# A routed expert stage on one core: second products spread between the next steps' first products, results added one step later

## Chip, cores and metric

The kernel runs on one NeuronCore of a Trainium2 chip. The metric is the device time of one launch in microseconds (us), the median of several runs. Lower is better.

## What is computed

A two-layer graph network on 1250 nodes with 1024 features is followed by a feed-forward layer in which each row is sent to 2 of 8 experts. The change touches the experts alone. Cut to that part, the reference is:

```python
def _L0_ffn_ref(x, rw1, rb1, rw2, rb2, ew1, eb1, ew2, eb2):
    B, F, D, H, E, K = (4, 256, 1024, 256, 8, 2)
    t = x.reshape(b * f, d)
    logits = silu(t @ rw1 + rb1) @ rw2 + rb2
    vals, idx = top_k(logits, K)
    ...
    w = softmax(masked, axis=1)
    eh = silu(einsum('td,edh->teh', t, ew1) + eb1[None])
    eo = einsum('teh,ehd->ted', eh, ew2) + eb2[None]
    y = t + einsum('te,ted->td', w, eo)
```

The kernel computes eh and eo only for the two chosen experts of each row.

## The kernel before

The rows are sorted by expert into blocks of 128 slots. The stage takes 17 steps (NS). A step belongs to one expert and has two blocks (a big step, 256 rows wide) or one (a small step, 128 rows wide). The fixed list ORDER makes steps 0, 3, 5, 8, 11, 13 and 16 small and the ten others big. BLOCKS(s) is the number of blocks of step s, WIDE(s) its width. Almost every tile has two buffers, chosen by u = s % 2.

Each float32 factor is split into a high part, which ScalarE copies out, and a low part, which VectorE gets by subtraction; a product is then three matmuls: high by high, high by low, low by high. One step s is made of these parts:

- Loading: SyncE's queue loads the first weights (w_raw, w = 0) and the second ones (w = 1), 1 MB each, as soon as the low parts of step s-2 free the buffer (m_wlo). GpSimd's queue gathers the rows (x_rows, L2093) when the transposes of step s-2 are done (m_tx), and issues the scatters (L2086) that add o_rows of a step to the output. There the gather of step t stands behind the scatter of step t-5.
- Splitting the weights: w1_hi (ScalarE, L2176; it waits until the first products of step s-2 are done, m_g1) and w1_lo (VectorE, L2226); w2_hi (ScalarE, L2181) and w2_lo (VectorE, L2226 too).
- Turning (turn, L2118): 8 transposes for each block on TensorE, in four groups, into PSUM banks 0 and 1. ScalarE copies a group to xt_hi (L2186) and VectorE forms xt_lo (L2231), after which the bank is free (m_xlo), so that group 2 waits for xt_lo of group 0.
- First products (L2132): for each half j of the 256 hidden columns 24 matmuls into bank 2 + j. ScalarE makes hid of them (L2194), then hid_hi (L2201), and VectorE hid_lo (L2249).
- Second products (tail of TensorE, L2153): 12 matmuls of 512 columns for each block, in two groups of 6, each into a PSUM bank of its own (4 + 2b + half). A group of step s waits on m_out until VectorE has read the bank's result of step s-1.
- Results: ScalarE's shift writes the weighted bias into o_rows (L2210), once for each block, and VectorE adds the scaled bank to it (L2259), once for each group, which counts up m_out.

Each engine's order is written out by hand. The pipeline runs head(s) and then tail(s-1). On TensorE head(s) is: 24 first products, half of the transposes of step s+1, 24 first products, the other half; tail(s-1) is the block of second products. On ScalarE head(s) is w1_hi of step s+1, hid of half 0, two groups of xt_hi, w2_hi of step s, hid of half 1, two groups of xt_hi, hid_hi; then follows shift(s-1). On VectorE head(s) is w1_lo of step s+1, two groups of xt_lo, w2_lo of step s, two groups of xt_lo, hid_lo; then the results of step s-1. Before and among the first transposes TensorE runs matmuls whose results nobody reads (keep_busy, L1976).

Of the kernel before, what the change touches and what calls it, by code (L numbers as in the profile page):

```python
# [31 lines left out]
KT = D // 128  # L32
# [29 lines left out]
M = 256  # L62
SUB = M // 128
BIG, SMALL = 10, 7
NS = BIG + SMALL
# [12 lines left out]
HK = HID // 128  # L78
# [25 lines left out]
def build(nc, I, out):  # L104
    ctx = ExitStack()
    with ctx:
# [1924 lines left out]
        LATE = 5  # L2031
        w1_view, w2_view = I["L0_ffn_ew1"], I["L0_ffn_ew2"]
# [70 lines left out]
        def _(e):  # L2103
# [6 lines left out]
            def turn(s, u, q, groups=range(4)):  # L2110
                if groups[0] == 0:
                    for b in range(BLOCKS(s)):
                        e.wait_ge(m_xin[u][b], NTH(s, b))
                for g in groups:
                    e.wait_ge(m_xlo, 4 * s + g + 1)
                    for k in range(2):
                        for b in range(BLOCKS(s)):
                            mm = e.transpose(ps[:, g % 2, k * M + 128 * b:k * M + 128 * b + 128],  # L2118
                                             x_rows[:, u, b, 128 * (2 * g + k):128 * (2 * g + k + 1)], ident[:])
                    mm.then_inc(m_tx, 1)  # L2120


            def head(s, u, q):
                e.wait_ge(m_wlo[0], s + 3)
                e.wait_ge(m_xlo, 4 * s + 4 + 2)
                for j in range(HK):
                    e.wait_ge(m_h, HK * s + j + 1)
                    n = 0
                    for k in range(KT):
                        for wt, xt in ((w1_hi, xt_hi), (w1_hi, xt_lo), (w1_lo, xt_hi)):  # L2130
                            n += 1
                            mm = e.matmul(ps[:, 2 + j, 0:WIDE(s)], wt[:, u, k, 128 * j:128 * j + 128], xt[:, u, k, 0:WIDE(s)],  # L2132
                                          start=(n == 1), stop=(n == 3 * KT))
                    mm.then_inc(m_g1, 1)
                    if not isinstance(s, int) or s < NS - 1:
                        turn(s + 1, 1 - u, q + u, range(2 * j, 2 * j + 2))
                if s == 0:
                    slot_weights(e)

            def tail(s, u, q):  # L2140
                if s == 1:
                    e.wait_ge(g_sl, 1)
                e.wait_ge(m_hlo, s + 1)
                e.wait_ge(m_wlo[1], s + 3)
                for b in range(BLOCKS(s)):
                    for half in range(2):
                        if s > 0:
# [159 lines left out]
```

## Time and profile before

| what | value |
|---|---|
| median of 3 runs | 1111.09 us |
| lowest and highest run | 1102.71 and 1113.34 us |
| span of the profiled execution, first to last instruction | 1107.6 us |
| difference between the median and that span | 3.5 us |
| mean granted TensorE clock in the span | 0.989 |
| the expert stage in it, from the first transpose (889.7 us) to the end | 217.9 us |

The page gives no time of the profiled execution beside its span. The rows further on come from this execution. A stretch is given in us from the start of the span. PE is TensorE, ACT ScalarE, DVE VectorE, POOL GpSimd, SP SyncE. The end of a matmul in the trace is modelled, so the distance from one start to the next is what it costs TensorE; "2.87 us x24" in the chain of waits is such a distance for 24 in a row.

### The profile page before, as it was taken

The page shows a single profiled execution, that of the slowest core. Times are in us where ns is not written, and L with a number is a line of the kernel's source. Part 1 is how long each engine was busy: PE and PEld are TensorE (multiplying, and loading weights), DVE is VectorE, ACT ScalarE, POOL GpSimd, SP SyncE. Part 2 cuts the span into 40 slices and gives each one's busy share as a digit, 9 for nine tenths or more (in the row PEclk, how much of TensorE's full clock was granted, in tenths as well). Part 3 has the DMA queues.
Part 4 walks back from the last instruction along what each step waited for, and adds up shares of the span by engine and source line. Part 5 has one row for each costly group of instructions (what it writes and reads, how often), then busy time and mean ns, then how long its engine had stood idle before and what let it go on. Part 6 is the DMA issues. An engine that isn't in the chain of part 4 may idle for free.

```text
span 1107.6 us, 18245 instructions
## 1 busy us (share of the span) xinstructions
PE 1068.1 (96%) x6565; PEld 1015.3 (92%) x6565; DVE 618.0 (56%) x1090; ACT 427.1 (39%) x934; POOL 193.4 (17%) x192
## 2 busy tenths in 40 slices
PE   5999999999999999999999999999999989999995
PEld 4999999999999999999999999999999679999994
DVE  6678888888752344334323523273222467878883
ACT  5555434453311222121121112164322257777672
POOL 5500000000000002000200020002442124555532
PEclk9999999999999999999999999999999979999998
DMA  6332133213227560004201430276565187999971
GB/s 191 95 105 71 44 108 108 70 43 105 71 71 242 148 186 16 1 19 150 67 1 54 129 76 1 58 244 189 158 186 190 38 302 233 318 304 291 304 220 29
DMA packets 72794, 144.97 MB, mean 131 GB/s; under 512 B 12822, under 2 KB 51667, under 8 KB 68209
## 3 DMA queue, kind: packets, MB, share of 16 engines
q1 hardware_dynamic: 61041, 112.50, 31.7%
q0 software_dynamic: 10976, 30.74, 10.7%
q8 instruction: 68, 1.11, 0.4%
q10 hardware_dynamic: 672, 0.32, 0.1%
q14 instruction: 37, 0.30, 0.1%
HBM read 108.40 MB, written 42.96 MB: 137 GB/s over the span
## 4 chain that ended last, share of the span: by engine, by line
PE 91%; DVE 3%; issue 2%; DMA 1%; DVEq 1%; ACT 1%; POOLq 0%; SPq 0%; POOL 0%; ACTq 0%
PE ps L1482 20%; PE ps L976 14%; PE ps L1554 10%; PE ps L2132 9%; PE ps L1521 9%; PE ps L1211 8%; PE ps L2153 6%; PE ps L821 4%; PE ps L735 3%; PE ps L2118 2%; PE ps L716 1%; DVE key_hot L814 1%; PE ps L921 1%; PE ps L1540 1%; DVE adj L828 1%
## 5 line engine op out<-in xcount | busy, mean ns | idle before, releaser
L1444 POOL TENSOR_TENSOR s_rows<-s_rows,b1t 125x1368 f32<-125x1368 f32 (+3 forms) x9 | 23.7, 2655 | 572.1 <-DMA s_rows<-in_x 572.1
L828 DVE TENSOR_TENSOR adj<-ps,adj 125x250 f32 x212 | 87.7, 414 | 42.0 <-PE ps L821 33.7
L976 PE MATMUL ps<-h_lo,w_hi 128*128 128x418 f32 x336 | 108.6, 372 | 0.0
L976 PE MATMUL ps<-h_hi,w_hi 128*128 128x418 f32 x336 | 100.3, 379 | 0.0
L1521 PE MATMUL ps<-z_hi,adj 125*125 125x342 f32 (+1 forms) x300 | 95.0, 322 | 1.4 <-DVE s_rows L1753 1.4
L1521 PE MATMUL ps<-z_lo,adj 125*125 125x342 f32 (+1 forms) x300 | 94.3, 319 | 0.0
L976 PE MATMUL ps<-h_hi,w_lo 128*128 128x418 f32 x336 | 93.4, 359 | 0.0
L2226 DVE TENSOR_TENSOR w_lo<-w_raw,w_hi 128x2048 fp32r<-128x2048 f32 x34 | 77.8, 2288 | 25.6 <-ACT w_hi L2181 20.8
L1211 PE MATMUL ps<-adj,y_hi 125*128 125x416 f32 (+1 forms) x240 | 85.8, 357 | 2.2 <-DVE layer_out L1276 1.6
L1211 PE MATMUL ps<-adj,y_lo 125*128 125x416 f32 (+1 forms) x240 | 85.4, 356 | 0.0
L821 PE MATMUL ps<-key_hot,src_hot 125*125 125x250 bf16 x424 | 80.8, 271 | 3.4 <-DVE adj L828 3.1
L2132 PE MATMUL ps<-xt_hi,w_hi 128*128 128x256 f32 (+1 forms) x272 | 78.4, 288 | 0.2
L2132 PE MATMUL ps<-xt_lo,w_hi 128*128 128x256 f32 (+1 forms) x272 | 77.5, 285 | 0.0
L2132 PE MATMUL ps<-xt_hi,w_lo 128*128 128x256 f32 (+1 forms) x272 | 77.5, 285 | 0.0
L1482 PE MATMUL ps<-wn_hi,hs_lo 128*125 128x342 f32 (+1 forms) x240 | 76.7, 320 | 0.0
L1482 PE MATMUL ps<-ws_hi,hs_hi 128*125 128x342 f32 (+1 forms) x240 | 76.7, 320 | 0.0
L1482 PE MATMUL ps<-wn_hi,hs_hi 128*125 128x342 f32 (+1 forms) x240 | 76.7, 320 | 0.0
L1482 PE MATMUL ps<-ws_lo,hs_hi 128*125 128x342 f32 (+1 forms) x240 | 76.7, 319 | 0.0
L1482 PE MATMUL ps<-ws_hi,hs_lo 128*125 128x342 f32 (+1 forms) x240 | 76.6, 319 | 0.0
L1482 PE MATMUL ps<-wn_lo,hs_hi 128*125 128x342 f32 (+1 forms) x240 | 76.5, 319 | 0.0
L821 PEld LDWEIGHTS ps<-key_hot,src_hot 125*125 125x125 bf16 x424 | 56.5, 136 | 18.7 <-issue 7.0
L814 DVE TENSOR_TENSOR key_hot<-seq,key_now 125x1000 bf16<-125x1000 f16 x106 | 71.2, 672 | 0.0
(301 smaller groups left out, 2685.6 us busy)
## 6 DMA issues: line engine op xcount, KB each, us to landing
w_raw<-in_L_ffn_ew SPq DMA_DIRECT2D x34, 1024.0 KB
xin<-in_x SPq DMA_DIRECT2D x10, 448.0 KB
t_d<-xn SPq DMA_DIRECT2D x10, 448.0 KB
base<-x_d POOLq DMA_DIRECT2D x10, 448.0 KB, 4.2
out<-base POOLq DMA_DIRECT2D x10, 448.0 KB, 3.5
y_d<-y_hi SPq DMA_DIRECT2D x7, 625.0 KB
y_d<-y_lo SPq DMA_DIRECT2D x7, 625.0 KB
self_d<-self SPq DMA_DIRECT2D x7, 625.0 KB
```

Source lines behind the costliest of these rows:

```text
L735: mm = e.matmul(FIRST_BANK(own, c)[:, a - COLS[c][0]:b - COLS[c][0]], wt[:, own, k, :], ht[:, k, a:b], start=(n == 0), stop=(n == 3 * KT - 1))
L814: ins = e.tensor_tensor(both(hot).rearrange("p c (v x) -> p c v x", x=2), seq, place, ALU.is_equal)
L821: mm = e.matmul(ps[0:P, 5 + b % 2, 0:KW], src_hot[:, b, g, 0:P], key_hot[:, b, g, :], start=(g == 0), stop=(g == G - 1))
L828: e.tensor_tensor(cols, ps[0:P, 5 + b % 2, 0:KW].rearrange("p (t w) -> p t w", t=NT), cols, ALU.add).then_inc(self.took, 1)
L976: mm = e.matmul(BANK(m, own, c), wt[:, own, k, :], ht[:, k, a:a + w], start=(k == 0 and p == 0), stop=(k == KT - 1 and p == 2))
L1211: mm = e.matmul(ps[:, banks[c], 0:w], y[:, k, :], adj_[:, k, a:a + w], start=(n == 1), stop=(n == 2 * NT))
L1482: mm = e.matmul(ps[0:P, 2 * v + u, 0:w], ht[:, u, k, :], wt[v][:, k, 0:w], start=(k == EARLY[0] and p == 0), stop=(k == LATE_K[-1] and p = ...
L1521: mm = e.matmul(ps[0:P, 2 + n % 2, 0:w], adj_[:, k, tile_of(j)], z[:, k, 0:w], start=(k == 0 and p == 0), stop=(k == NT - 1 and p == 1))
L1554: mm = e.matmul(ps[:, i % 5, 0:w], wt[u][:, k, :], ht[:, k, a:a + w], start=(n == 1), stop=(n == 3 * KT))
L2132: mm = e.matmul(ps[:, 2 + j, 0:WIDE(s)], wt[:, u, k, 128 * j:128 * j + 128], xt[:, u, k, 0:WIDE(s)], start=(n == 1), stop=(n == 3 * KT))
L2153: mm = e.matmul(ps[:, 4 + 2 * b + half, :], ht[:, u, j, 128 * b:128 * b + 128], wt[:, u, j, 512 * half:512 * half + 512], start=(n == 1), ...
L2226: e.tensor_tensor(lo[:, u], raw[:, u], hi[:, u].bitcast(F32), ALU.subtract).then_inc(m_wlo[i], 1)
```

## The change

On TensorE the two functions head and tail give way to single matmuls that are dealt out in turn. Iteration t has two phases of 24 first products of step t. In phase 0 (half j = 0) the second half of the second products of step t-2 is spread evenly between them. In phase 1 (j = 1) come the 16 or 8 transposes of step t+1, spread over the first 20 of the 24, and the first half of the second products of step t-1, spread over all 24. HALF(s) is 12 matmuls for a big step and 6 for a small one. Two more iterations at the end hold the second products that are left. The semaphore that each group of second products waits on (m_out) is the same as before. The first products of half 0 now wait for xt_lo group by group.

On VectorE the results of a step (outputs, formerly tail) are added one step later, inside head: after w1_lo of step s+1 and ahead of all four groups of xt_lo. w2_lo of step s comes behind the four groups. On ScalarE all four groups of xt_hi of step s+1 come behind hid of half 0, ahead of w2_hi of step s and hid of half 1. The queues of SyncE and GpSimd keep their order.

```diff
@@ -2029,6 +2029,7 @@
         NTH = lambda s, b: 16 * sum(i % 2 == s % 2 and b < BLOCKS(i) for i in range(s + 1))
         WIDE = lambda s: 128 * BLOCKS(s)
         LATE = 5
+        PRODUCTS, TURNING = 3 * KT, 20
         w1_view, w2_view = I["L0_ffn_ew1"], I["L0_ffn_ew2"]
 
         def gated(e):
@@ -2107,57 +2108,81 @@
             e.sem_inc(m_g1, 4)
             e.sem_inc(m_g2, 2 * NB)
 
-            def turn(s, u, q, groups=range(4)):
-                if groups[0] == 0:
-                    for b in range(BLOCKS(s)):
-                        e.wait_ge(m_xin[u][b], NTH(s, b))
-                for g in groups:
+            def turned(s, i):
+
+                u, B = s % 2, BLOCKS(s)
+                g, r = divmod(i, 2 * B)
+                k, b = divmod(r, B)
+                if i == 0:
+                    for c in range(B):
+                        e.wait_ge(m_xin[u][c], NTH(s, c))
+                if r == 0:
                     e.wait_ge(m_xlo, 4 * s + g + 1)
-                    for k in range(2):
-                        for b in range(BLOCKS(s)):
-                            mm = e.transpose(ps[:, g % 2, k * M + 128 * b:k * M + 128 * b + 128],
-                                             x_rows[:, u, b, 128 * (2 * g + k):128 * (2 * g + k + 1)], ident[:])
+                mm = e.transpose(ps[:, g % 2, k * M + 128 * b:k * M + 128 * b + 128],
+                                 x_rows[:, u, b, 128 * (2 * g + k):128 * (2 * g + k + 1)], ident[:])
+                if r == 2 * B - 1:
                     mm.then_inc(m_tx, 1)
 
-
-            def head(s, u, q):
-                e.wait_ge(m_wlo[0], s + 3)
-                e.wait_ge(m_xlo, 4 * s + 4 + 2)
-                for j in range(HK):
+            def product(s, j, n):
+
+                u = s % 2
+                k, p = divmod(n, 3)
+                wt, xt = ((w1_hi, xt_hi), (w1_hi, xt_lo), (w1_lo, xt_hi))[p]
+                if n == 0:
+                    e.wait_ge(m_wlo[0], s + 3)
                     e.wait_ge(m_h, HK * s + j + 1)
-                    n = 0
-                    for k in range(KT):
-                        for wt, xt in ((w1_hi, xt_hi), (w1_hi, xt_lo), (w1_lo, xt_hi)):
-                            n += 1
-                            mm = e.matmul(ps[:, 2 + j, 0:WIDE(s)], wt[:, u, k, 128 * j:128 * j + 128], xt[:, u, k, 0:WIDE(s)],
-                                          start=(n == 1), stop=(n == 3 * KT))
+                if j == 0 and n % 6 == 0:
+                    e.wait_ge(m_xlo, 4 * s + n // 6 + 1 + 2)
+                mm = e.matmul(ps[:, 2 + j, 0:WIDE(s)], wt[:, u, k, 128 * j:128 * j + 128], xt[:, u, k, 0:WIDE(s)],
+                              start=(n == 0), stop=(n == PRODUCTS - 1))
+                if n == PRODUCTS - 1:
                     mm.then_inc(m_g1, 1)
-                    if not isinstance(s, int) or s < NS - 1:
-                        turn(s + 1, 1 - u, q + u, range(2 * j, 2 * j + 2))
-                if s == 0:
+
+            def second(s, i):
+
+                u = s % 2
+                group, n = divmod(i, 3 * HK)
+                b, half = divmod(group, 2)
+                j, p = divmod(n, 3)
+                ht, wt = ((hid_hi, w2_hi), (hid_hi, w2_lo), (hid_lo, w2_hi))[p]
+                if i == 0:
+                    if s == 1:
+                        e.wait_ge(g_sl, 1)
+                    e.wait_ge(m_hlo, s + 1)
+                    e.wait_ge(m_wlo[1], s + 3)
+                if n == 0 and s > 0:
+                    e.wait_ge(m_out, GROUP_AT(s - 1) + 2 * NB + min(group + 1, 2 * BLOCKS(s - 1)))
+                mm = e.matmul(ps[:, 4 + group, :], ht[:, u, j, 128 * b:128 * b + 128],
+                              wt[:, u, j, 512 * half:512 * half + 512], start=(n == 0), stop=(n == 3 * HK - 1))
+                if n == 3 * HK - 1:
+                    mm.then_inc(m_g2, 1)
+
+            def share(n, of, total):
+
+                return range(min(n, of) * total // of, min(n + 1, of) * total // of)
+
+            HALF = lambda s: 3 * HK * BLOCKS(s) if 0 <= s < NS else 0
+            for i in range(8 * BLOCKS(0)):
+                turned(0, i)
+                if i == 4 * BLOCKS(0) - 1:
+                    keep_busy(e, 5)
+            keep_busy(e, 4)
+            for t in range(NS + 2):
+                turns = 8 * BLOCKS(t + 1) if t + 1 < NS else 0
+                for n in range(PRODUCTS):
+                    if t < NS:
+                        product(t, 0, n)
+                    for i in share(n, PRODUCTS, HALF(t - 2)):
+                        second(t - 2, HALF(t - 2) + i)
+                for n in range(PRODUCTS):
+                    if t < NS:
+                        product(t, 1, n)
+                    for i in share(n, TURNING, turns):
+                        turned(t + 1, i)
+                    for i in share(n, PRODUCTS, HALF(t - 1)):
+                        second(t - 1, i)
+                if t == 0:
                     slot_weights(e)
-
-            def tail(s, u, q):
-                if s == 1:
-                    e.wait_ge(g_sl, 1)
-                e.wait_ge(m_hlo, s + 1)
-                e.wait_ge(m_wlo[1], s + 3)
-                for b in range(BLOCKS(s)):
-                    for half in range(2):
-                        if s > 0:
-                            e.wait_ge(m_out, GROUP_AT(s - 1) + 2 * NB + min(2 * b + half + 1, 2 * BLOCKS(s - 1)))
-                        n = 0
-                        for j in range(HK):
-                            for ht, wt in ((hid_hi, w2_hi), (hid_hi, w2_lo), (hid_lo, w2_hi)):
-                                n += 1
-                                mm = e.matmul(ps[:, 4 + 2 * b + half, :], ht[:, u, j, 128 * b:128 * b + 128],
-                                              wt[:, u, j, 512 * half:512 * half + 512], start=(n == 1), stop=(n == 3 * HK))
-                        mm.then_inc(m_g2, 1)
-            turn(0, 0, 0, range(0, 2))
-            keep_busy(e, 5)
-            turn(0, 0, 0, range(2, 4))
-            keep_busy(e, 4)
-            skewed(e, NS, head, tail)
 
         def more(s):
             return not isinstance(s, int) or s < NS - 1
@@ -2192,9 +2217,9 @@
                 for j in range(HK):
                     wait_apart(e, m_g1, HK * s + j + 1 + 4)
                     e.activation(hid[:, u, j, 0:WIDE(s)], ps[:, 2 + j, 0:WIDE(s)], ACT.Silu, bias=eb1c[:, ds(x * HK + j, 1)]).then_inc(m_h, 1)
-                    if more(s):
-                        rows(s + 1, 1 - u, q + u, range(2 * j, 2 * j + 2))
                     if j == 0:
+                        if more(s):
+                            rows(s + 1, 1 - u, q + u)
                         w2(s, u, q)
                 e.wait_ge(m_h, HK * s + HK + 2)
                 e.wait_ge(m_g2, GROUP_AT(s - 1) + 2 * NB)
@@ -2241,16 +2266,17 @@
             def head(s, u, q):
                 if more(s):
                     w(0, w1_raw, w1_hi, w1_lo, s + 1, 1 - u, q + u)
-                    rows(s + 1, 1 - u, q + u, range(0, 2))
+                if s >= 2:
+                    outputs(s - 2, u)
+                if more(s):
+                    rows(s + 1, 1 - u, q + u)
                 w(1, w2_raw, w2_hi, w2_lo, s, u, q)
-                if more(s):
-                    rows(s + 1, 1 - u, q + u, range(2, 4))
                 e.wait_ge(m_hhi, s + 1)
                 e.tensor_tensor(hid_lo[:, u, :, 0:WIDE(s)], hid[:, u, :, 0:WIDE(s)], hid_hi[:, u, :, 0:WIDE(s)].bitcast(F32), ALU.subtract).then_inc(m_hlo, 1)
                 if s == 0:
                     slot_sums()
 
-            def tail(s, u, q):
+            def outputs(s, u):
                 for b in range(BLOCKS(s)):
                     e.wait_ge(m_eb, BLOCKS_TO(s) + b + 1)
                     for half in range(2):
@@ -2261,7 +2287,10 @@
             w(0, w1_raw, w1_hi, w1_lo, 0, 0, 0)
             rows(0, 0, 0)
             slot_shares(e)
-            skewed(e, NS, head, tail)
+            for s in range(NS):
+                head(s, s % 2, s // 2)
+            for s in range(NS - 2, NS):
+                outputs(s, s % 2)
 
 
         @on("sync")
```

TensorE around the start of the second products of step 1. m_out is the wait on VectorE's results. Before, they stand in one block behind both halves of the first products of step 2 (L2132) and all transposes of step 3 (L2118):

```order
L2132 MATMUL ps<-xt_hi,w_lo 128x256
L2118 MATMUL ps<-ident,x_rows 128x128 [waits m_xlo]
L2118 MATMUL ps<-ident,x_rows 128x128
L2118 MATMUL ps<-ident,x_rows 128x128 [waits m_xlo]
L2118 MATMUL ps<-ident,x_rows 128x128
L2153 MATMUL ps<-w_hi,hid_hi 128x512 [waits m_wlo1,m_out,m_hlo,g_sl]
L2153 MATMUL ps<-w_lo,hid_hi 128x512
```

Now the first of them (L2155) stands behind only two of the 24 first products of half 1 of step 2 (L2136; the one that waits on m_h is the first of the 24):

```order
L2136 MATMUL ps<-xt_hi,w_lo 128x256
L2155 MATMUL ps<-w_hi,hid_lo 128x512
L2136 MATMUL ps<-xt_hi,w_hi 128x256 [waits m_h,m_wlo0]
L2136 MATMUL ps<-xt_lo,w_hi 128x256
L2155 MATMUL ps<-w_hi,hid_hi 128x512 [waits m_wlo1,m_out,m_hlo,g_sl]
L2136 MATMUL ps<-xt_hi,w_lo 128x256
L2121 MATMUL ps<-ident,x_rows 128x128 [waits m_xlo,m_xin10]
L2136 MATMUL ps<-xt_hi,w_hi 128x256
L2155 MATMUL ps<-w_lo,hid_hi 128x512
```

What has moved: 22 first products and all transposes of that iteration now stand behind this wait instead of ahead of it.

VectorE, one step. Before, from the results of step 1 (two blocks, four additions L2259, each of which counts up m_out) to the xt_lo of the next step (L2231):

```order
L2249 TENSOR_TENSOR hid_lo<-hid,hid_hi 128x512 [waits m_hhi]
L2259 SCALAR_TENSOR_TENSOR o_rows<-ps,slot_w,o_rows 128x512 [waits m_g2,m_eb]
L2259 SCALAR_TENSOR_TENSOR o_rows<-ps,slot_w,o_rows 128x512 [waits m_g2]
L2259 SCALAR_TENSOR_TENSOR o_rows<-ps,slot_w,o_rows 128x512 [waits m_g2,m_eb]
L2259 SCALAR_TENSOR_TENSOR o_rows<-ps,slot_w,o_rows 128x512 [waits m_g2]
L2226 TENSOR_TENSOR w_lo<-w_raw,w_hi 128x2048 [waits m_whi0]
L2231 TENSOR_TENSOR xt_lo<-ps,xt_hi 128x512 [waits m_xhi] x2
```

Now the same additions (L2285), behind w1_lo, which waits for w1_hi of ScalarE (m_whi0):

```order
L2251 TENSOR_TENSOR w_lo<-w_raw,w_hi 128x2048 [waits m_whi1]
L2275 TENSOR_TENSOR hid_lo<-hid,hid_hi 128x512 [waits m_hhi]
L2251 TENSOR_TENSOR w_lo<-w_raw,w_hi 128x2048 [waits m_whi0]
L2285 SCALAR_TENSOR_TENSOR o_rows<-ps,slot_w,o_rows 128x512 [waits m_g2,m_eb]
L2285 SCALAR_TENSOR_TENSOR o_rows<-ps,slot_w,o_rows 128x512 [waits m_g2]
L2285 SCALAR_TENSOR_TENSOR o_rows<-ps,slot_w,o_rows 128x512 [waits m_g2,m_eb]
L2285 SCALAR_TENSOR_TENSOR o_rows<-ps,slot_w,o_rows 128x512 [waits m_g2]
L2256 TENSOR_TENSOR xt_lo<-ps,xt_hi 128x512 [waits m_xhi] x4
```

What has moved: one w1_lo now stands between hid_lo and the additions.

ScalarE now, from hid of half 0 (L2219) to the next w1_hi (L2201); before, two of the four xt_hi stood behind hid of half 1:

```order
L2219 ACTIVATE hid<-ps,eb1c 128x256
L2211 ACTIVATE xt_hi<-ps 128x2x128 [waits m_tx] x4
L2206 ACTIVATE w_hi<-w_raw 128x2048 [waits m_g2,m_win10]
L2219 ISA [waits m_g1]
L2219 ACTIVATE hid<-ps,eb1c 128x256
L2226 ACTIVATE hid_hi<-hid 128x512 [waits m_g2,m_h]
L2229 TENSOR_LOAD step_x
L2229 ISA x2
L2235 ISA [waits m_kept]
L2235 ACTIVATE o_rows<-eb_all,slot_w 128x1024
L2214 TENSOR_LOAD step_x
L2201 ACTIVATE w_hi<-w_raw 128x2048 [waits m_g1,m_win00]
```

What has moved: w2_hi (L2206) now stands behind the last xt_hi and ahead of hid of half 1.

## Rows read from the trace of the kernel before

**Rows 1.** The page, busy time, and the granted clock in 40 slices
```profile
PE 1068.1 (96%) x6565; PEld 1015.3 (92%) x6565; DVE 618.0 (56%) x1090; ACT 427.1 (39%) x934; POOL 193.4 (17%) x192
...
PEclk9999999999999999999999999999999979999998
```
**Rows 2.** Chain of waits in order of time: start us, us, what
```profile
893.66 2.87 PE ps L2132 x24
896.52 3.26 issue
899.78 1.94 PE ps L2118 x8
...
955.28 2.63 PE ps L2132 x24
957.91 0.90 PE ps L2118 x8
958.80 2.63 PE ps L2132 x24
...
962.33 5.49 PE ps L2153 x24
...
974.45 0.87 PE ps L2118 x8
975.33 2.77 PE ps L2153 x12
978.10 2.87 PE ps L2132 x24
```
**Rows 3.** ACT in order of time, one step
```profile
984.49 0.48 ACT L2194 ACTIVATE hid<-ps,eb1c 128x256 f32<-128x256 f32 x1 [0.48 <-PE ps L2132]
984.86 0.65 ACT L2186 ACTIVATE xt_hi<-ps 128x256 fp32r<-128x256 f32 x2
985.39 0.64 ACT L2201 ACTIVATE hid_hi<-hid 128x512 fp32r<-128x512 f32 x1
985.91 2.20 ACT L2210 ACTIVATE o_rows<-eb_all,slot_w 128x1024 f32 x2
987.99 1.92 ACT L2176 ACTIVATE w_hi<-w_raw 128x2048 fp32r<-128x2048 f32 x1
993.05 0.37 ACT L2194 ACTIVATE hid<-ps,eb1c 128x128 f32<-128x128 f32 x1 [3.13 <-PE ps L2132]
993.33 1.09 ACT L2186 ACTIVATE xt_hi<-ps 128x512 fp32r<-128x512 f32 x2
994.30 1.92 ACT L2181 ACTIVATE w_hi<-w_raw 128x2048 fp32r<-128x2048 f32 x1
```
**Rows 4.** DVE in order of time, one step
```profile
987.51 2.19 DVE L2259 SCALAR_TENSOR_TENSOR o_rows<-ps,slot_w,o_rows 128x512 f32<-128x512 f32 x3
990.24 0.75 DVE L2259 SCALAR_TENSOR_TENSOR o_rows<-ps,slot_w,o_rows 128x512 f32<-128x512 f32 x1 [0.54 <-PE ps L2153]
990.91 2.28 DVE L2226 TENSOR_TENSOR w_lo<-w_raw,w_hi 128x2048 fp32r<-128x2048 f32 x1
993.96 1.29 DVE L2231 TENSOR_TENSOR xt_lo<-ps,xt_hi 128x512 fp32r<-128x512 f32 x2 [0.77 <-ACT xt_hi L2186]
```
**Rows 5.** Stretches: us, busy PE, PEld, DVE, ACT, POOL, PEclk, DMA share, GB/s
```profile
347.00:353.00 6.00, 6.00 (x26) 5.79 (x26) 0.00 (x0) 0.00 (x0) 0.00 (x0) 0.72 0.88 255
896.50:899.80 3.30, 0.04 (x2) 0.05 (x1) 3.30 (x4) 0.37 (x1) 0.00 (x0) 0.74 0.80 305
899.80:914.00 14.20, 14.14 (x87) 13.91 (x88) 8.62 (x11) 6.66 (x8) 0.99 (x1) 0.58 0.80 298
1020.00:1040.00 20.00, 20.00 (x133) 18.16 (x132) 17.04 (x20) 13.73 (x17) 9.55 (x6) 1.00 1.00 310
```
**Rows 6.** PE in order of time, ahead of the first of these falls
```profile
344.99 2.34 PE L1259 MATMUL ps<-ones,dinv_row 1*125 1x1 f32 x20
```
**Rows 7.** Who waited for whom from 870 us: us in total, times, longest us
```profile
POOL x_rows L2093 <- PE ps L2118: 53.7, 15, 13.4
```
**Rows 8.** POOL in order of time, last scatter
```profile
1098.03 1.56 POOL L2086 DMA_INDIRECT out<-o_rows,ids_i  x1 [2.08 <-DMA out<-o_rows,ids_i]
```

## Prediction

> **What bounds the kernel now.** I read the page first: TensorE is busy for 96% of the span, at the full clock in all slices but one [rows 1]. The chain of waits then shows the expert stage as TensorE's work end to end. A big step is 24 first products in 2.87 us (0.12 each), twice; 8 transposes in 0.87 to 0.90 (0.11 each), twice; and second products in 0.23 each, 24 in 5.49 or 12 in 2.77. In a small step 24 first products take 2.63 [rows 2]. From 914 us to the last product this goes on without a gap. The only real hole in the stage is 3.26 us at 896.52, before the first transposes of step 1 [rows 2]. So TensorE is the bound, and the change neither adds nor removes a matmul. It can win only if mixing makes the same matmuls cheaper, and it can lose wherever an in-order wait comes too early. ScalarE and VectorE have waits today, but the reader should look at how long their chain from one step to the next is, not at their busy shares.
>
> The transfers are the other resource that is nearly full: a DMA share of 1.00 at 310 GB/s between 1020 and 1040 us [rows 5]. The change moves no issue on SyncE's or GpSimd's queue, but their releases come with VectorE's and TensorE's work. GpSimd waits for transposes for 53.7 us in 15 times [rows 7], so the gathers have room, and if steps get longer all loads get more. I count them at nothing. If that cover went, the price would be a wait like the 3.26 us one.
>
> **What the change makes late.** Call zero of iteration t the end of the last first product of step t-1. In phase 1 the first second product of step t-1 stands behind two first products (four, if t-1 is small) and waits on m_out for the first result of step t-2. VectorE adds that result only behind w1_lo of step t+1; that needs w1_hi of step t+1, which ScalarE does behind hid half 1 and hid_hi of step t-1 and the bias rows of step t-2. Before, the same bank had been read a whole step earlier in VectorE's order, and the block of second products (5.49 us) gave this chain its room.
>
> The chain, from starts to next starts: hid to hid_hi, with its own write to wait for, 0.5; hid_hi to bias rows 985.39 to 985.91, 0.52; bias rows 985.91 to 987.99, 1.04 a block; w1_hi 1.92 [rows 3]; w1_lo 2.25, first addition 0.75 [rows 4]; handing over 0.1. That is 6.05 + 1.04 per block of step t-2.
>
> It starts late as well. ScalarE's w2_hi now stands between the last xt_hi and hid half 1. The last transpose stands behind the 20th first product. From its end ScalarE needs 0.2 to start, 0.49 for xt_hi of a big step (993.33 to 994.30 for two) or 0.27 of a small one (984.86 to 985.39 for two), and 1.9 for w2_hi [rows 3]. TensorE meanwhile has 4 first products and 3 (or 2, if step t-2 is small) second ones left: 4 x 0.12 + 3 x 0.23 = 1.16, 1.12 after a small t-1, or 0.94 with two. So hid half 1 starts 1.2 to 1.65 after zero.
>
> TensorE reaches the wait after phase 0 (24 first products and 12 or 6 second ones) and a few matmuls of phase 1. Steps 2 to 15 fall into five kinds, by the blocks of steps t-2, t-1, t, t+1:
>
> - 1,2,2,1 (4 times). Result at 1.65 + 6.05 + 1.04 = 8.75. TensorE there at 2.87 + 1.38 + 0.24 = 4.5. Wait 4.25.
> - 2,2,1,2 (3 times). 1.2 + 6.05 + 2.08 = 9.35 against 2.63 + 2.77 + 0.33 = 5.7. Wait 3.65.
> - 2,1,2,1 (twice). 1.47 + 8.13 = 9.6 against 2.87 + 2.77 + 0.59 = 6.2. Wait 3.4.
> - 1,2,1,2 (twice). 1.43 + 7.09 = 8.5 against 2.63 + 1.38 + 0.33 = 4.3. Wait 4.2.
> - 2,1,2,2 (3 times). 9.6 against 2.87 + 2.77 + 0.81 = 6.45. Wait 3.15.
>
> Sum: 17.0 + 10.95 + 6.8 + 8.4 + 9.45 = 52.6 us. Queued behind the waiting product are 20 to 22 first products and all transposes of the iteration, and ScalarE waits for these in turn; nothing of the wait is regained.
>
> A second wait follows where step t-2 has two blocks. Four additions (0.7 each, 2.8) now stand ahead of xt_lo, and the transposes of group 2 need xt_lo of group 0. In the last kind xt_lo of group 0 is done at about 12.2 and TensorE is there at 11.5: 0.75 more. In the third kind it is 0.35, in the others nothing. That is 3 x 0.75 + 2 x 0.35 = 3.0.
>
> **Edits that cost little.** Waiting for xt_lo group by group takes no time that the transposes have not spent. Start: the hole before step 1 stays, with two first products moved ahead of it; at the half clock these are 0.4, and the first xt_lo of step 2 comes a little late, so I take -0.3 (bounds -0.5 and +1). End: step 16 waits for no w1. The last additions and scatters come closer together: scatter of step 15 at about 5.7 after the end of the first products, landed 2.7 later, last scatter at 9.3. Today the last scatter starts 10.8 after that point (1087.19 to 1098.03, [rows 8]), but 12 more second products, 2.77, lie in it. So 12.0 against 10.8, +1.2 (bounds 0 and +2).
>
> What the trace does not show is a 128-column transpose or product next to a 512-column one. If each of the 324 second products hid the part of a neighbour that does not grow with its columns (0.11 less a quarter of 0.23, 0.053), this would give 17 us; if each of about 27 changes of width in a step cost 0.02, 17 steps would lose 9. The nearest rows, the change from transposes to second products in the chain, show neither (8 and 24 in 0.90 and 5.49), so I take 0. Where TensorE waits anyway, a gain in phase 0 is only more waiting.
>
> **The clock.** The 3.26 us hole was enough to bring the granted clock from 2.4 to 1.2 GHz: 0.74 in the hole, 0.58 in the 14.2 us behind it [rows 5], which costs 0.42 x 14.2 = 6.0. A shorter lull did it as well: 2.3 us of matmuls of one column [rows 6] left a clock of 0.72 over the next 6 us [rows 5], 1.7 us lost. Each of the 14 waits is 3.15 to 4.25 us, as long as that hole. Behind it come wide matmuls, as in the cheaper of the two cases, not the narrow ones of step 0. So I take 14 x 1.7 = 24, with 0 and 14 x 6.0 = 84 as ends. What is slow in phase 0 of the next iteration costs nothing, since TensorE would wait there.
>
> The Trainium skill, "TensorE: Matmul & The Clock Gate", section "HAM oscillation — how this bites in real kernels", says that a wait between bursts of matmuls, repeated in a loop, lets the clock drop each time and makes each burst begin cold. By that rule the 24 us belong to the sum; without it the sum ends at the waits alone. The two falls above agree with it; no row here shows the repetition.
>
> **Sum.** 52.6 + 3.0 - 0.3 + 1.2 = 56.5, with the clock 80.3. The profiled span of 1107.6 becomes 1187.9. The median of the runs is 3.5 above that span, and I add the same: 1111.1 + 80.3 = 1191.4, say 1191 us.
>
> **The rivals.**
>
> 1. The clock holds. The same waits, but too short or too broken for the chip to act on. For it: from 914 us on the clock is full. Against it: the hole of 3.26 us. Time: 1111.1 + 56.5 = 1168. Chance 0.22.
> 2. The clock falls and stays down for long, as behind the hole of step 0. For it: four of seven small steps have many narrow matmuls behind the wait. Against it: second products of 512 columns lie between them. Time: 1168 + 84 = 1252. Chance 0.10.
> 3. The change does not do this: the wait on m_out is met, since VectorE's additions come earlier than I work out, and TensorE stays full with the same matmuls. It needs a chain 3 to 4 us shorter than its rows. Time: within 1% of before. Chance 0.06.
> 4. Faster: narrow next to wide. A 128-column matmul takes 0.11, though its columns are a quarter of those of a 0.23 one, so something else than streaming holds it. Laid next to a second product, that rest could vanish beside the long one. Price: 324 x 0.053 = 17 us, at full effect 1094. It decides only if the wait on m_out falls under about 1 us a step; above that the gain in phase 0 goes into the wait. Chance 0.05.
>
> On the fourth: the Trainium skill, same page, section "Step-by-step: what each phase is for", states that the load of the next weights is pulled ahead of matmuls in flight. By this rule the load for a narrow matmul behind a wide one is hidden. The rows of before have it hidden in the blocks too, so the rule alone does not say which order is better.
>
> My forecast has 0.57. The range is 1150 to 1222 us: the low end is the first rival with most of the gain of the fourth, the high end the forecast with falls of 4 us each in place of 1.7. It leaves out the second rival and most of the last two. About 1% is what a measurement of this kernel can tell from no change; by that bound: faster 0.05, same 0.06, slower 0.89.
>
> **What would show it.** In the trace of after, the longest wait of TensorE should be that of second products (L2155) for the additions (L2285), some 53 us in 14 times, each 3 to 4.3 us; matmuls as long as before at the full clock; hid half 1 (L2219) behind w2_hi (L2206) without a gap, 1.2 to 1.7 us after the first products end; a granted clock below 1.00 in most iterations; a DMA share clearly under 1.00; a big-step iteration of 16 to 19 us, where it was 13. I am wrong on the mechanism if TensorE has no such wait, wrong on the clock if it stays at 1.00 from 914 us on, and wrong on the mixing if starts in phase 0 lie closer than 0.12 and 0.23.

## The result and the profile after

| | before | after |
|---|---|---|
| median | 1110.3 us (4 runs) | 1184.32 us (4 runs, 1182.55 to 1185.62) |
| span of the profiled execution | 1107.6 us | 1182.3 us |
| mean granted clock | 0.989 | 0.967 |

The ratio is 1.0681, with a 95% interval of 1.0646 to 1.0715: 7% slower, inside the range, 7 us under the predicted time. The profiled span is 5.6 us under the predicted 1187.9; the rest is that the median lies 2.0 us above the span here, not 3.5.

The page of after, busy times and the clock in 40 slices, to be held against [rows 1]:

```profile
PE 1090.2 (92%) x6565; PEld 1031.7 (87%) x6565; DVE 622.9 (53%) x1090; ACT 433.0 (37%) x934; POOL 172.4 (15%) x192
...
PEclk9999999999999999999999999999998899889888
```

The number of matmuls is the same, their busy time has grown by 22 us, and the clock is now broken in the expert stage, the last ten slices.

Who waited for whom on PE from 910 to 1150 us (us in total, times, longest):

```profile
PE ps L2155 <- DVE o_rows L2285: 50.8, 14, 4.3
PE ps L2121 <- DVE xt_lo L2256: 1.1, 1, 1.1
```

This is the forecast wait, in every one of steps 2 to 15. Its length goes by the kind of step. In the prediction's order of kinds: 4.1 to 4.2 (said 4.25), 3.5 (3.65), 3.1 (3.4), 4.2 to 4.3 (4.2), 2.9 to 3.2 (3.15).

One of them, step 7, in the order of PE (start us, us; in brackets the idle time ahead and what ended it):

```profile
1002.53 0.28 PE L2136 MATMUL ps<-xt_hi,w_hi 128*128 128x256 f32 x1
1002.65 0.28 PE L2136 MATMUL ps<-xt_lo,w_hi 128*128 128x256 f32 x1
1007.06 0.47 PE L2155 MATMUL ps<-w_hi,hid_hi 128*128 128x512 f32 x1 [4.13 <-DVE o_rows L2285]
1007.37 0.28 PE L2136 MATMUL ps<-xt_hi,w_lo 128*128 128x256 f32 x1
```

ACT and DVE up to that point:

```profile
997.53 0.60 ACT L2211 ACTIVATE xt_hi<-ps 128x512 fp32r<-128x512 f32 x1 [0.68 <-PE ps L2121]
998.02 1.91 ACT L2206 ACTIVATE w_hi<-w_raw 128x2048 fp32r<-128x2048 f32 x1
999.83 0.46 ACT L2219 ACTIVATE hid<-ps,eb1c 128x256 f32<-128x256 f32 x1
1000.33 0.63 ACT L2226 ACTIVATE hid_hi<-hid 128x512 fp32r<-128x512 f32 x1
1000.98 1.16 ACT L2235 ACTIVATE o_rows<-eb_all,slot_w 128x1024 f32 x1
1002.04 1.89 ACT L2201 ACTIVATE w_hi<-w_raw 128x2048 fp32r<-128x2048 f32 x1
```

```profile
1003.96 2.29 DVE L2251 TENSOR_TENSOR w_lo<-w_raw,w_hi 128x2048 fp32r<-128x2048 f32 x1 [1.11 <-ACT w_hi L2201]
1006.17 1.40 DVE L2285 SCALAR_TENSOR_TENSOR o_rows<-ps,slot_w,o_rows 128x512 f32<-128x512 f32 x2
```

Read from the top: the last xt_hi, w2_hi, hid without a gap (so it came late), hid_hi, bias rows, w1_hi, w1_lo, addition, and 0.14 us after its end the matmul. That is the chain of [rows 3, 4], now with nothing beside it.

Three stretches of after (columns as in [rows 5]). The middle one goes from inside the first long wait, which ends at 923.47 us, to 6.5 us behind the end of the last:

```profile
904.00:921.00 17.00, 13.92 (x102) 12.73 (x101) 11.54 (x14) 12.62 (x15) 2.54 (x3) 1.00 0.59 206
921.00:1149.00 228.00, 178.91 (x1071) 162.61 (x1072) 127.96 (x138) 113.21 (x140) 54.80 (x41) 0.87 0.67 196
1149.00:1182.30 33.30, 19.27 (x114) 16.31 (x112) 13.33 (x16) 12.06 (x14) 9.54 (x5) 0.85 0.18 25
```

TensorE is busy for 78% of the middle stretch, at 0.87 of the clock, and the DMA share is 0.67; in the kernel before it is 0.93 from 921 to 1081.7 us, with the 1.00 of [rows 5] as its fullest part. The record of the granted clock has 14 falls to one half there, one at each of the 14 waits (it begins inside the wait or within 1.2 us of its end): ten of 3.4 us and four of 6.8 us.

### The profile page after: what moved, and what is told of

The parts are those of the page before. It is cut to its first block, busy times and chain, and to the rows that moved or that the text cites. A ratio compares the mean times of both kernels' runs of the same rounds, so it can differ in the third digit from the quotient of the medians.

```text
span 1182.3 us, 18262 instructions
## 1 busy us (share of the span) xinstructions
PE 1090.2 (92%) x6565; PEld 1031.7 (87%) x6565; DVE 622.9 (53%) x1090; ACT 433.0 (37%) x934; POOL 172.4 (15%) x192
## 4 chain that ended last, share of the span: by engine, by line
PE 78%; issue 7%; DVE 5%; ACT 5%; DMA 2%; DVEq 1%; ACTq 1%; POOLq 0%; SPq 0%; POOL 0%
PE ps L1482 19%; PE ps L976 13%; PE ps L1554 9%; PE ps L1521 8%; PE ps L1211 7%; PE ps L2155 4%; PE ps L2136 4%; PE ps L821 4%; PE ps L735 3%; PE ps L2121 2%; ACT w_hi L2201 2%; ACT o_rows L2235 1%; DVE o_rows L2285 1%; DMA out<-o_rows,ids_i 1%; PE ps L716 1%
## 5 line engine op out<-in xcount | busy, mean ns | idle before, releaser
L2155 PE MATMUL ps<-w_hi,hid_hi 128*128 128x512 f32 x108 | 51.8, 479 | 51.4 <-DVE o_rows L2285 51.2
L2136 PE MATMUL ps<-xt_hi,w_hi 128*128 128x256 f32 (+1 forms) x272 | 82.4, 303 | 0.0
L2136 PE MATMUL ps<-xt_hi,w_lo 128*128 128x256 f32 (+1 forms) x272 | 82.1, 302 | 0.0
L2136 PE MATMUL ps<-xt_lo,w_hi 128*128 128x256 f32 (+1 forms) x272 | 81.9, 301 | 0.0
L2211 ACT ACTIVATE xt_hi<-ps 128x512 fp32r<-128x512 f32 (+1 forms) x68 | 34.5, 510 | 124.8 <-PE ps L2121 124.8
```

The lines of the kernel that those rows point to most:

```text
L2155: mm = e.matmul(ps[:, 4 + group, :], ht[:, u, j, 128 * b:128 * b + 128], wt[:, u, j, 512 * half:512 * half + 512], start=(n == 0), stop=(n ...
L2211: e.activation(group(xt_hi, s, u, g), bank(s, g), ACT.Copy).then_inc(m_xhi, 1)
```

## The experiments

Each time is a median, each ratio is to the kernel before on the same chip. All kernels do all the work unless a text says otherwise.

**The addition ahead of the split.** On VectorE:

```diff
             def head(s, u, q):
+                if s >= 2:
+                    outputs(s - 2, u)
                 if more(s):
                     w(0, w1_raw, w1_hi, w1_lo, s + 1, 1 - u, q + u)
-                if s >= 2:
-                    outputs(s - 2, u)
                 if more(s):
                     rows(s + 1, 1 - u, q + u)
```

> The changed kernel with one edit on VectorE: in each step the results of step s-2 are added ahead of w1_lo of step s+1, not behind it. Nothing is left out. Theory (the new wait is an in-order one, TensorE on the first addition, which stands behind w1_lo and so behind ScalarE's w1_hi): the first addition then needs only the bias rows, the 14 waits of L2155 of 2.9 to 4.3 us (50.8 us) fall under 0.5 us each, and the clock stays at 1.00 behind the start. What is late next is xt_lo of group 0, now behind w1_lo: about 1 us in most steps, 12 us in all. Time 1184 - 51 - 28 (clock) + 12 = 1118 us, 1112 to 1124. Rival A (dealing out the second products singly costs TensorE time by itself, in switching between widths and banks): the time stays over 1150 with TensorE busy. Rival B (mixing hides loads of narrow matmuls, which only the waits covered up): under 1100.

Measured: 1122.11 us, ratio 1.0128 (1.0094 to 1.0162). PE's waits from 910 us on:

```profile
PE ps L2121 <- DVE xt_lo L2256: 9.8, 11, 1.2
PE ps L2155 <- DVE o_rows L2284: 4.6, 7, 0.7
```

One exchange of places on VectorE takes back 62 of the 74 us. The wait for xt_lo that the theory names as next is there, and behind the start the clock no longer falls. The time is inside the expected range, 4 us over its middle: six waits of 0.7 us on additions are left where I said under 0.5, and one of 0.3 near the end.

**w2_hi back between the groups of xt_hi.** On ScalarE:

```diff
                         if more(s):
-                            rows(s + 1, 1 - u, q + u)
+                            rows(s + 1, 1 - u, q + u, range(0, 2))
                         w2(s, u, q)
+                        if more(s):
+                            rows(s + 1, 1 - u, q + u, range(2, 4))
```

> The changed kernel with one edit on ScalarE: w2_hi of a step stands again between the second and the third group of xt_hi, not behind the fourth. Nothing is left out. Theory (the chain starts late because hid of half 1 stands behind w2_hi): hid starts about 0.2 us after the last first product in place of 1.2 to 1.65, so each of the 14 waits is 1.0 to 1.4 us shorter: 51 becomes about 33 us. The clock then falls at some of them; 1146 to 1161 us, about 1153. Rival (the wait is VectorE's own, its order or its load, and ScalarE's place doesn't matter): waits still over 48 us, time within 5 us of 1184.

Measured: 1164.28 us, ratio 1.051 (1.0469 to 1.0552), 3 us above the expected range; PE's waits on additions 38.7 us, where I said 33. In the three kinds in which step t-2 has two blocks they are 1.7 to 2.5 us, as expected. In the other two they are 3.7 to 3.8 but for the first, only 0.4 shorter than in after. The chain of waits of this kernel shows why, at the hid of one of these steps:

```profile
993.99 0.49 ACT hid L2219
994.48 0.02 issue
994.50 0.63 ACT hid_hi L2228
995.13 0.61 ACTq L2231
...
996.10 0.48 ACT o_rows L2237
```

ACTq is ScalarE's own instruction queue. Line 2231 reads the expert's number into a register (TENSOR_LOAD) ahead of the bias rows. Its shortest, median and longest time in this kernel, in ns:

```profile
L2231 ACTq TENSOR_LOAD <-step_x x17: 273/282/1276, 917.6 to 1145.2; - x17
```

The load starts with hid_hi, here and in after. In after it takes 0.28 us in most steps and is over before hid_hi is. Here it takes 1.2 to 1.3 us in five steps, those of the two kinds but for the first, and the bias rows start 1.6 us behind hid_hi in place of 0.65. ScalarE waits for TensorE ahead of this hid in the other kinds too, so that is not what makes the load long; what does, no run shows. So ScalarE's place is part of the chain, worth 1.7% here (1.0681 to 1.051, with four falls of the clock fewer), and the rival falls; but the chain has a piece that is not the same in every kernel.

The clock falls at 10 of the 14 waits, and not simply at the longest. Two stretches of this kernel, the first around a wait of 3.71 us, the second around one of 1.89 us (PEclk is the third figure from the end):

```profile
1047.00:1055.00 8.00, 5.79 (x39) 5.37 (x40) 3.99 (x6) 3.23 (x5) 1.61 (x1) 1.00 0.89 305
1078.00:1086.00 8.00, 6.12 (x34) 5.61 (x33) 5.24 (x8) 3.39 (x6) 3.19 (x2) 0.79 0.81 244
```

**The waits filled.** On TensorE, ahead of phase 1:

```diff
+                for n in range(24 if 2 <= t < NS - 1 else 0):
+                    if n == 0:
+                        e.wait_ge(m_h, HK * t + 2)
+                        e.wait_ge(m_wlo[0], t + 3)
+                    e.matmul(ps[:, 3, 0:WIDE(t)], w1_hi[:, t % 2, 0, 128:256], xt_hi[:, t % 2, 0, 0:WIDE(t)],
+                             start=True, stop=True)
```

> The changed kernel with 24 extra matmuls on TensorE ahead of phase 1 in steps 2 to 15 (a first product into the bank that the next one starts anew), 2.9 us in a big step, 2.6 in a small one. All work that counts is kept, in its order. Theory (14 waits make the clock fall 14 times, which costs 28 us beside the waits): the extra matmuls lie inside the waits, which shrink to 0.3 to 1.6 us each (12 us in all), the result comes no later, and the clock holds at 1.00: 1184 - 28 = 1156 us, 1150 to 1162. Rival (the falls of the clock cost nothing on the path, since what bounds a step is the chain on ScalarE and VectorE): 1184 us, or 1222 if the extra matmuls add to the path.

Measured: 1168.07 us, ratio 1.0554 (1.0518 to 1.0591). PE's waits, and the clock:

```profile
PE ps L2155 <- DVE o_rows L2291: 14.2, 13, 2.6
```

```profile
919.00:1130.00 211.00, 196.24 (x1401) 181.03 (x1400) 128.23 (x139) 113.54 (x141) 58.37 (x41) 0.98 0.72 211
```

With 336 matmuls more the kernel is 16 us faster: the falls do cost time on the path, and the rival falls. Two falls are left, behind the two longest remaining waits (2.09 and 2.58 us); in these two steps the register load took 1.0 and 1.5 us. But 28 us was too much: the time is 6 us above the expected range. From the end of the first long wait to that of the last it is 203.4 us in this trace and 219.0 in that of after: 15.6 us for 11 falls fewer in that stretch, about 1.4 each. A fall costs TensorE rather more than that, since part of the gain was lost again: in steps 6 and 14 the fill used up the whole wait, and over the stretch waits and fill together are some 2 us longer (12.6 and an estimated 36.1) than the 46.6 us of waits in after.

**Both exchanges together.**

> The edits of e1_results_first and e2_w2_between together. Nothing is left out. Theory: with hid in time w1_hi and w1_lo are 1.2 us earlier, so that the wait for xt_lo of group 0 remains only where step s-2 has two blocks: about 6 us in all. Time 1112 us, 1107 to 1118: no faster than before, since TensorE does the same matmuls at the same distances. Rival B (mixing hides loads): under 1100. Rival A (mixing costs by itself): over 1130.

Measured: 1118.59 us, ratio 1.0096 (1.0058 to 1.0135), 0.6 us above the expected range. PE's waits:

```profile
PE ps L2121 <- DVE xt_lo L2258: 8.0, 11, 1.1
PE ps L2155 <- DVE o_rows L2286: 0.3, 1, 0.3
```

The waits on additions are gone, but for one near the end. The ones for xt_lo stay in four of the five kinds of steps, not only behind two blocks: VectorE cannot start w1_lo before the last addition, and this one waits for the last second product of phase 0.

**w1_lo between the groups of xt_lo too.**

```diff
                 if more(s):
+                    rows(s + 1, 1 - u, q + u, range(0, 2))
                     w(0, w1_raw, w1_hi, w1_lo, s + 1, 1 - u, q + u)
-                    rows(s + 1, 1 - u, q + u)
+                    rows(s + 1, 1 - u, q + u, range(2, 4))
```

> The kernel of e4_both_orders with w1_lo of step s+1 on VectorE moved from ahead of the first to between the second and the third group of xt_lo. Nothing is left out. With this the new order of TensorE runs with hardly a wait and so shows what dealing out the second products is worth by itself. Theory (same matmuls at the same distances, no gain in mixing): the 10 waits of L2121 of 0.6 to 1.1 us (7.6 us) go, 1118.6 - 8 = 1111 us, 1106 to 1115, the same as before within 0.7%. Rival B (mixing hides loads of narrow matmuls): 1095 or less. Rival A (mixing costs by itself): it stays at 1117 or more with TensorE busy.

Measured: 1110.38 us, ratio 1.0036 (1.0011 to 1.006). PE's waits from 910 us on, and the stretch up to the last products:

```profile
PE ps L2121 <- DVE xt_lo L2258: 0.8, 1, 0.8
PE ps L2155 <- DVE o_rows L2287: 0.3, 1, 0.3
```

```profile
914.00:1087.00 173.00, 171.98 (x1191) 156.11 (x1189) 136.38 (x151) 126.77 (x156) 79.22 (x44) 1.00 0.90 270
```

This is the new order of TensorE with its waits taken away: full clock, no holes, and by the interval 0.1 to 0.6% slower than before. Both rivals on mixing fall. Dealing out wide matmuls between narrow ones gains nothing and costs little. From the first product of step 2 to the last product it is 178.1 us here (912.12 to 1090.24), 1.2 of them waits. In the kernel before it is 174.0 us (921.08 to 1095.07), with six second products fewer (1.4 us) in it. That leaves 1.6 us for the mixing. The rest of the 4 us between the medians does not show in the two traces.

In big steps the single distances are nearly those of the blocks. In small steps they shift, and the sum stays:

```profile
923.25 0.22 PE L2136 MATMUL ps<-xt_hi,w_hi 128*128 128x128 f32 x1
923.31 0.27 PE L2136 MATMUL ps<-xt_lo,w_hi 128*128 128x128 f32 x1
923.42 0.45 PE L2155 MATMUL ps<-w_hi,hid_hi 128*128 128x512 f32 x1
923.71 0.22 PE L2136 MATMUL ps<-xt_hi,w_lo 128*128 128x128 f32 x1
```

The four starts are 0.06, 0.11 and 0.29 apart, 0.46 in all; in blocks they would be 0.11, 0.11 and 0.23, 0.45 in all.

This trace also prices a fall of the clock. TensorE does the same matmuls in it as in after. From the first second product of step 1 to that of step 14 it takes 150.2 us here, 0.8 of it a wait. In after it takes 219.0 us, from the end of the first long wait to that of the last. Of the 69.6 us between 219.0 and 149.4, 46.6 are the 13 waits; 23 are left for the 13 falls, 1.8 each.

**The hole at the start of the stage filled, in the kernel before.** The same 24 matmuls, 128 wide, between the first products of half 0 of step 0 and the transposes of step 1.

> The kernel before with 24 extra matmuls on TensorE in step 0, between the first products of half 0 and the first transposes of step 1 (a first product into the bank of half 1, which is started anew later), about 2.7 us in the hole of 3.26 us. All work that counts is kept. Theory (the hole makes the clock fall, which costs 6.0 us in the 14.2 us behind it): the clock stays at 1.00 there and the kernel gains 4 to 6 us: 1107 - 5 = 1102 us. Rival (a fall there costs nothing that the next waits would not take): 1107 us, as before.

Measured: 1109.16 us, ratio 1.0008 (0.9977 to 1.0038): the expected 4 to 6 us are not there, at most 2.5. Over all runs the mean granted clock did rise, from 0.990 to 0.993 (medians), and the chain of waits shows 4 us won where they were expected. The kernel before, behind the hole, and this one:

```profile
901.72 5.01 PE ps L2132 x24
...
909.92 3.92 PE ps L2132 x24
```

```profile
896.27 2.68 PE ps L2138 x24
898.95 0.90 PE ps L2118 x8
899.85 2.63 PE ps L2132 x24
902.48 0.90 PE ps L2118 x8
903.38 0.77 PE ps L2006 x20
904.15 1.81 issue
905.97 3.10 PE ps L2132 x24
```

The first products of step 1 start at 905.97 in place of 909.92. The last product of the stage starts at 1094.75 and started at 1095.07. In between PE has a wait that the kernel before did not have:

```profile
PE ps L2118 <- issue: 2.9, 1, 2.9
```

It is a transpose at 1060.38 us, whose rows had been gathered by an issue at 1058.43 that stood on GpSimd's queue behind a scatter; that scatter had waited 8.39 us for the one before it to land. That wait was followed by a fall of the clock of 3.4 us as well. Together they account for the 3.6 us by which the way from the first products of step 1 to the last product is longer than before. Behind the last product another 2.9 us are lost: 15.4 us to the end, where it was 12.5, in a chain of scatters that wait for one another. So in this execution the gain was given back to late transfers, in the stage and at its end.

**The same in the mixed order.**

> e7_w1_between with the same 24 extra matmuls in step 0, ahead of phase 1. Nothing is left out. Theory: the clock was at the half for 3.4 to 6.8 us there in the kernels of this order, so 2 to 3 us are won against e7_w1_between; the time is that of e6_before_filled within 5 us. Rival: no difference to e7_w1_between.

Measured: 1109.93 us, ratio 1.0028 (1.0007 to 1.0049), no difference to the kernel without it, as the rival said. Here a load of first weights came 4.0 us late for ScalarE (2.5 us in the kernel without the fill), TensorE waited 2.3 us for xt_lo behind it, and the clock fell for 3.4 us.

**Half the weight traffic.** From step 3 on each load brings half of its tile:

```diff
+                part = (KT, HK)[w] // (2 if s >= 3 else 1)
-                e.dma_start(raw[:, u], view[ds(x, 1)].rearrange("a p k n -> p (a k) n")).then_inc(m_win[w][u], 16)
+                e.dma_start(raw[:, u, 0:part], view[ds(x, 1)].rearrange("a p k n -> p (a k) n")[:, 0:part]).then_inc(m_win[w][u], 16)
```

In the kernel before with the hole filled:

> The kernel of e6_before_filled in which, from step 3 on, each weight load brings only half of its tile (0.5 MB in place of 1 MB); the other half keeps what was there, so the experts' results are left incomplete, with all matmuls and splits as before. Theory (the 4 us that the filled hole gains at the start are given back because weights and gathers land late, the transfers being as full as TensorE): without that traffic the gain stays: 1107 - 5 = 1102 us, and TensorE has no wait behind step 1. Rival (the gain was never one, or is lost at the end of the kernel): 1106 to 1109, as e6_before_filled.

Measured: 1105.84 us, ratio 0.9984 (0.9966 to 1.0002). The trace is as the theory says: no wait of TensorE behind step 1, the last product at 1091.11, 4 us earlier than in the kernel before, and 12.5 us from there to the end. But the median is 4 us above the expected 1102, only 1 us below before, and the interval holds 1. Inconclusive: the late transfers are shown, that they are the whole of what is given back is not.

In the kernel before, and in the changed one:

> The kernel before with the same half loads from step 3 on, so that the experts' results are left incomplete. Theory (TensorE bounds the kernel before, which had no wait for a transfer behind step 1 in its trace): 1104 to 1107 us, about as before. Rival (the transfers bound it already): 1100 or less.

Measured: 1106.91 us, ratio 0.999 (0.9971 to 1.0009). The kernel before is not held up by its transfers.

> The changed kernel with the same half loads from step 3 on, so that the experts' results are left incomplete. Theory (its 14 waits are for the chain on ScalarE and VectorE, not for transfers): 1182 to 1186 us, the waits of 2.9 to 4.3 us unchanged. Rival (the waits come from late weights): 1150 or less.

Measured: 1186.44 us, ratio 1.0719 (1.0679 to 1.0759), with the 14 waits at the same 2.9 to 4.3 us. The time is 0.4 us above the expected range, and the interval overlaps that of after. Half the weight traffic changes nothing that can be told: the rival falls. That the DMA share of 0.67 in after comes from the longer steps fits this.

**Gathers further ahead.** The kernel with the filled hole, and LATE = 6:

> The kernel of e6_before_filled with LATE = 6: on GpSimd's queue the gather of step t stands behind the scatter of step t-6, not t-5. Nothing is left out. Theory (the late transfer that gives the gain back is a gather queued behind a scatter that waits for the one before it): the gathers are issued earlier, 1102 to 1105 us. Rival (all transfers together are too many, whatever their order): 1106 to 1109.

Measured: 1134.55 us, ratio 1.025 (1.0217 to 1.0282), a plain miss. Who waited for whom from 915 us on:

```profile
ACT o_rows L2215 <- POOLq L2083: 45.1, 11, 9.5
DVE o_rows L2264 <- ACT o_rows L2215: 39.0, 9, 9.1
...
PE ps L2118 <- DVE xt_lo L2236: 15.7, 5, 6.1
```

Line 2083 is the count m_kept, which GpSimd raises at a scatter and on which the bias rows of the next step wait. I had looked at which gather is issued earlier, not at who waits for the scatter that is issued later.

## Why the prediction came out right

**The mechanism and the 52.6 us.** The 14 waits sum to 50.8 us. The exchange on VectorE alone removes them but for 4.6 us, the one on ScalarE shortens them, half the weight traffic leaves them as they are. The step that works out when the result is there and when TensorE is there holds to 0.3 us for each kind, and its pieces hold too: hid of half 1 starts 1.1 to 1.6 us after zero (said 1.2 to 1.65).

**The second wait, 3.0 us, did not come.** Only one wait for xt_lo is in the trace of after, 1.1 us, in step 1. This term was sized too large. With the waits filled VectorE has the same order and the clock is full in these steps, and there the second wait is 0.3 us in the three steps of the last kind (said 0.75) and nothing in the third kind (said 0.35). In after TensorE comes to these transposes from a stretch at the half clock, and finds the bank free. The 8 to 10 us of waits for xt_lo in the kernels with the additions ahead of w1_lo are another wait: there w1_lo stands between the additions and xt_lo.

**The clock, 24 us.** All 14 waits brought it down, as the prediction took it, and as the rule of the Trainium skill that it cites ("TensorE: Matmul & The Clock Gate", section "HAM oscillation — how this bites in real kernels") has it; this case's trace now shows the repetition, 14 of 14. The size holds as well: against the kernel with the waits removed a fall costs 1.8 us, some 25 us in all, where the prediction took 1.7. Taking falls away by filling the waits won 1.4 each. That the size fits so well is partly luck. The 1.7 came from a single fall in another part of the kernel, with 6.0 as the other choice, and the lull of [rows 6] that it followed stands in the trace of after too, where the clock stays full.

**Start and end, +0.9 us.** The hole before step 1 was 2.7 us (was 3.26) and the half clock behind it shorter, 6.8 us from its fall where it was 13.7, which the prediction did not foresee. From the first transpose to the first product of step 2 it is 26.7 us in place of 31.4, with six second products (1.4 us) fewer: 3.3 us won, outside the bounds of -0.5 and +1. This is one execution; the half clock at this place is 3.4 to 10.2 us long in the traces of the experiments that do not fill the hole. From the last product to the end it is 14.0 us, and was 12.5: +1.5 against +1.2.

**Mixing, 0 us.** Taken as nothing between -17 and +9; the kernel with the waits removed is at 1.0036, and its trace gives +1.6 us. The rule of the Trainium skill on weight loads being pulled ahead (same page, section "Step-by-step: what each phase is for"), which the prediction named beside its fourth rival, gives no gain by this order. Starts in phase 0 closer than 0.12 and 0.23 were to be a sign against the prediction. In small steps some are, at 0.06, but the next ones are as much further apart.

**Sum.** The spans differ by 74.7 us. The waits are 50.8 and the falls 25, the mixing is 1.6, the end 1.5 and a last wait 0.3. The start takes 3.3 back, and after reached its first transpose 1.8 us earlier (887.9 against 889.7), ahead of anything that the change touches. That makes 74.

**The rivals.** The clock did not hold (first), and no fall at a wait lasted past 6.8 us (second). The third and the fourth fall with the 14 waits and with the mixed order at 1.0036. The transfers, counted at nothing, do cost nothing in after. Their nearness shows elsewhere: with the full traffic, what the filled hole wins at the start is not in the median.

No kernel here beats the one before beyond its interval. The mixed order without its waits is 0.4% slower, at 1.0036.

## What to carry to other kernels

When work of an in-order engine is dealt out in finer pieces, look at each wait that travels with a piece: a wait that used to stand at the end of a step now stands at the head of everything behind it, and it is worth as much as the longest chain that feeds it. Work out that chain from one trace, start to start, across all engines, before counting busy shares; here it gave 14 waits to within 0.3 us. Where the order of one engine changes, the orders of the others have to follow: three exchanges of places on ScalarE and VectorE took a loss of 7% back to 0.4%.

## What the runs showed of the hardware that was not expected

- A wait of TensorE of 2.9 to 4.3 us brought the granted clock to one half in 14 of 14 cases, and again in 14 of 14 with half the weight traffic. With the waits filled two of 2.09 and 2.58 us did it as well. With w2_hi moved one of 1.89 us did and one of 3.71 us did not. The lull of [rows 6] stands in every trace; five of the 13 show a fall behind it. The hole of 1.8 us ahead of step 1 in the kernels before with the fill was followed by a fall in two of three. So the length of a wait alone does not decide.
- A microsecond at the half clock cost TensorE about 0.42 us (23 us for 55), and taking one away won about a third (15.6 us of path for 48 us less), part of the gain going into longer waits.
- Reading one number into a register on ScalarE's queue took 0.28 us in most steps of after and up to 1.3 and 1.5 us in a few of two experiments, on the same line of the program. Where it took long, the bias rows came up to 1.2 us later and TensorE with them. The cause is open.
- Dealing 512-column matmuls out between 128- and 256-column ones changed single distances (0.06 and 0.29 us in place of 0.11 and 0.23) and cost 1.6 us over some 175.
